# The direct term of the first half on VectorE, and the scan ahead of the second inverse chain: an S5 block on Trainium2

## The reference, cut to what matters

```python
x = x + _L0_conv_ref(_gn(x), ...)          # x: (16, 96, 16, 16), float32; _gn: 32 groups of 3 channels

def _L0_conv_ref(x, ...):
    u = x.reshape(Bsz, C, H * W).transpose(0, 2, 1)
    fx = _layernorm(u, ln1_g, ln1_b)                        # over the 96 channels
    res = fx
    ...                                                     # lam_bar, B_bar, masked Cc from 48 complex modes
    Bu = jnp.einsum('ph,blh->blp', B_bar, fx)
    _, xs = jax.lax.associative_scan(binop, (lam_el, Bu), axis=1)      # a linear recurrence over 256 positions
    y = 2.0 * jnp.real(jnp.einsum('hp,blp->blh', Cc, xs)) + D * fx
    y = jax.nn.gelu(y, approximate=False) + res
    fy = _layernorm(y, ln2_g, ln2_b)
    z = fy @ W_enc.T
    z1, z2 = jnp.split(z, 2, axis=-1)
    z = z1 * jax.nn.gelu(z2, approximate=False)
    y = z @ W_dec.T + fy
    return y.transpose(0, 2, 1).reshape(Bsz, C, H, W)
```

## Time and profile before

| | |
|---|---|
| median of 3 runs | 106.98 us |
| the profiled execution's own time | 106.55 us |
| its span, first to last instruction | 104.6 us |
| mean granted clock of TensorE | 0.991 |
| busy: PE, DVE, ACT, POOL | 95.2, 71.0, 43.8, 38.8 us |

### The profile page before, as it was taken

One profiled execution on the slowest core, in us unless ns is written; L12 is line 12 of the kernel. 1 busy time (PEld: TensorE's weight loads), 2 busy tenths in 40 slices (PEclk: granted clock), 3 DMA queues, 4 the chain that ended last, 5 costly groups with the idle time before them and its releaser, 6 DMA issues.

```text
span 104.6 us, 1481 instructions
## 1 busy us (share of the span) xinstructions
PE 95.2 (91%) x496; PEld 54.9 (52%) x496; DVE 71.0 (68%) x220; ACT 43.8 (42%) x93; POOL 38.8 (37%) x54
## 2 busy tenths in 40 slices
PE   5999789799999998898999999996899999999960
PEld 3667468274676654764775655674232533533300
DVE  1596995998670998585839113699950599994590
ACT  3420099999768001010292069254079322025200
POOL 7710465910599920000047000038992000495000
PEclk9999999999999999999999999999999999999996
DMA  2999100000000000000000000000000000550125
GB/s 76 250 247 217 24 0 0 0 6 0 3 0 0 0 0 6 0 0 0 0 3 0 0 0 0 6 0 0 0 0 0 0 0 0 150 151 6 51 79 171
DMA packets 3767, 3.79 MB, mean 36 GB/s; under 512 B 496, under 2 KB 3664, under 8 KB 3760
## 3 DMA queue, kind: packets, MB, share of 16 engines
q1 hardware_dynamic: 3504, 3.68, 13.8%
q10 hardware_dynamic: 256, 0.02, 0.2%
HBM read 2.12 MB, written 1.57 MB: 35 GB/s over the span
## 4 chain that ended last, share of the span: by engine, by line
PE 53%; DVE 19%; ACT 11%; DMA 6%; issue 5%; SPq 2%; DVEq 1%
PE ps L495 53%; DMA xs<-x_dram 6%; ACT xc L406 4%; ACT sq L406 3%; DVE w L744 3%; DVE rs L744 3%; ACT rotC L393 2%; DVE upper L748 2%; DVE fy L744 2%; SPq L247 1%; DVE rs L774 1%; DVE sq L744 1%; DVE st L783 1%; DVE y L1012 1%; DVE rs L749 1%
## 5 line engine op out<-in xcount | busy, mean ns | idle before, releaser
L343 POOL TENSOR_TENSOR y<-gl,fx 96x512 f32<-96x512 f32 x4 | 6.6, 1666 | 29.4 <-ACT gl L446 29.4
L495 PE MATMUL ps<-fy,mt 96*96 96x512 f32 x32 | 14.9, 599 | 1.3 <-DVE fy L744 1.3
L351 POOL TENSOR_TENSOR res<-fy,xs 96x512 f32<-96x512 f32 x8 | 10.7, 1354 | 11.6 <-DVE fy L744 11.5
L495 PE MATMUL ps<-wm 96*96 96x256 f32 x42 | 13.0, 467 | 1.2 <-DVE wm L980 1.2
L452 ACT ACTIVATE y<-ps,vecs 96x512 f32<-96x512 f32 x8 | 5.5, 685 | 16.5 <-PE ps L495 16.5
L744 DVE SCALAR_TENSOR_TENSOR w<-ps,vecs,y 96x512 f32<-96x512 f32 x8 | 5.9, 743 | 7.4 <-ACT y L452 7.4
L495 PEld LDWEIGHTS ps<-wm 96*96 96x96 f32 x42 | 8.2, 205 | 4.2 <-DVE wm L980 1.2
L495 PEld LDWEIGHTS ps<-fy,mt 96*96 96x96 f32 x32 | 5.0, 163 | 8.7 <-issue 6.9
L495 PE MATMUL ps<-xs,pm 96*96 96x256 f32 x32 | 8.5, 393 | 1.0 <-DVE pm L832 1.0
L744 DVE SCALAR_TENSOR_TENSOR w<-w,tb,ps 96x256 f32<-96x256 f32 x14 | 6.6, 472 | 3.8 <-ACT w L432 3.1
L495 PE MATMUL ps<-fx,dm 96*96 96x512 f32 x16 | 8.3, 602 | 0.4 <-DVE Z L880 0.4
(11 more groups left out here) (120 smaller groups left out, 161.9 us busy)
## 6 DMA issues: line engine op xcount, KB each, us to landing
out_dram<-sq SPq DMA_DIRECT2D x8, 192.0 KB, 2.2
xs<-x_dram SPq DMA_DIRECT2D x3, 384.0 KB, 6.5
xs<-x_dram SPq DMA_DIRECT2D x2, 192.0 KB, 2.9
mt<-mats_dram SPq DMA_DIRECT2D x1, 338.6 KB, 7.5
mt<-mats_dram SPq DMA_DIRECT2D x1, 180.0 KB, 5.2
sm<-small_dram ACTq DMA_DIRECT2D x1, 8.6 KB, 2.9
cmask<-mask_dram ACTq DMA_DIRECT2D x1, 9.0 KB, 3.1
```

What stands on the lines that cost most here:

```text
L343: nc.gpsimd.tensor_tensor(yv[:, RT * i:RT * (i + 1), :], cols(gl, H, i).rearrange("c (b m) -> c b m", b=RT), cols(fx, H, i).rearrange("c ( ...
L351: nc.gpsimd.tensor_tensor(cols(res, H, i), cols(fy, H, i), xs[:, HB * H + 2 * i:HB * H + 2 * i + 2, :].rearrange("c n l -> c (n l)"), ALU. ...
L495: return nc.tensor.matmul(o, lhsT, rhs, start=start, stop=stop)
```

## The change

Four edits. (1) A Sin activation of one column comes ahead of ScalarE's first copy. (2) `first_state(0)` moves ahead of the six centred copies. (3) The seven scan steps of the first half run in a row ahead of the second half's inverse chain. (4) The first half's four `direct` products go, the first local product of a tile now starts the accumulation, and `direct_term` on VectorE computes `fx * D + bank` into `gl`, from which Gelu then reads in place; the four multiply-adds stand among the second half's scan steps.

```diff
@@ -368,8 +370,9 @@
             act.dma_start(sm[:, :], small).then_inc(in_small, 16)
             act.dma_start(cmask[:, :], mask_in).then_inc(in_mask, 16)
+            act.wait_ge(wm_ready, 1)
+            nc.scalar.activation(sn[:, :], wm[:, 0:1], ACT.Sin)
             act.wait_ge(in_mask, 16)
@@ -442,8 +445,11 @@
                 act.wait_ge(db_ready, 1)
                 for i in range(NT):
-                    act.wait_ge(y_done, NT * H + i + 1)
-                    nc.scalar.activation(cols(gl, H, i), bank(H, i)[0:96, :], ACT.Gelu,
+                    if H:
+                        act.wait_ge(y_done, NT + i + 1)
+                    else:
+                        act.wait_ge(y_direct, i + 1)
+                    nc.scalar.activation(cols(gl, H, i), bank(H, i)[0:96, :] if H else cols(gl, H, i), ACT.Gelu,
                                          bias=db[:, 0:1]).then_inc(gl_ready, 1)
@@ -473,9 +479,9 @@
             squares(1, 4, HB)
-            centered_values(1, 2, HB)
             act.wait_ge(ones_ready, 2)
             first_state(0)
+            centered_values(1, 2, HB)
             seed(0)
@@ -605,7 +611,7 @@
                     mm(bank(H, i)[0:96, RC * j:RC * (j + 1)], yl[:, 0, b, :], rcols(w, H, b),
-                       start=False, stop=False)
+                       start=(H == 0 and j == 0), stop=False)
@@ -686,14 +692,14 @@
             for i in range(NT - 1):
-                direct(0, i)
+                pe.wait_ge(w_local[0], RT * (i + 1) - 1)
                 local_outputs(0, i)
...
-            direct(0, NT - 1)
+            pe.wait_ge(z_ready, NDBL)
             local_outputs(0, NT - 1)
@@ -878,6 +884,12 @@
+            def direct_term(i):
+
+                dve.wait_ge(y_done, i + 1)
+                stt(cols(gl, 0, i), cols(fx, 0, i), s(DD), bank(0, i)[0:96, :],
+                    ALU.mult, ALU.add).then_inc(y_direct, 1)
@@ -1015,9 +1027,10 @@
-            scan(0, 1)
-            scan(0, 2)
-            inverse_sigma(0, 1, lambda j: scan(0, j + 3) if 0 <= j < T - 3 else None)
+            for b in range(1, T):
+                scan(0, b)
+            inverse_sigma(0, 1)
+            dve.wait_ge(taken[0], 2 * HB)
             scale_tile(0, 1, 0, fx, s(G1), fx_ready)
@@ -1025,6 +1038,9 @@
             for b in range(1, T):
                 scan(1, b)
+                if b % 2 and b > 1:
+                    direct_term(b // 2 - 1)
+            direct_term(NT - 1)
             second_input(0, 1)
```

More of the change, by code:

```diff
@@ L122, in s5_block @@
         wm = sb("wm", [96, WARM_N])
+        sn = sb("sn", [96, 1])
         pm = sb("pm", [96, B, 96])
@@ L190, in s5_block @@
         y_done = sem("y_done")
+        y_direct = sem("y_direct")
         gl_ready = sem("gl_ready")
```

## The result

The changed kernel takes 108.15 us (median of 6 runs, 107.24 to 116.46), the kernel before 106.97 (6 runs, 106.52 to 109.21). The ratio is 1.0101, interval 1.0056 to 1.0146: slower by about 1%, by less than 2%. The profiled execution took 107.24 us, span 105.2, against 106.55 and 104.6.

A forecast was written before the change was run, and what follows sets the result against it. TensorE was taken as the main bound, with VectorE's chain setting the second half's broadcast. Chain gain -0.7 and multiply-adds +0.5 sum to -0.2 us, from 106.55 to 106.3 us; range 105.4 to 108.6.

The forecast's parts named there:

- rival A: TensorE's idle hole near 38 to 41 us lowers its clock: 2.0 us lost, 108.3 us in all; chance 0.30.
- the cost of the hole: Three direct products removed beside the chain save nothing; broadcast to last doubling stays 6.9 us at full clock.
- Table and first state: Front: one table load of 1.28 us goes, state copy moves ahead of six copies; first scan at 32.0, not 33.83.
- `rotS` near 24.1: Front: TensorE's `rotS` product starts 0.8 us earlier, near 24.1 instead of 24.95.
- Hold by GpSimd: Second inverse chain: its second link waits for GpSimd's last product in flight, until 37.47 as before.
- `parts` 41.15: Second inverse chain ends at 41.15 instead of 41.87, 3.68 us after the held second link.
- the term of -0.7: Gain of 0.7 us up to the end of the second inverse chain, from 41.87 to 41.15.
- The hole of 3.3 us: TensorE idles 3.3 us ahead of the second half's broadcast, near 37.9 to 41.2, where it idled 0.57.
- The multiply-adds, +0.5: First outputs: four VectorE multiply-adds among the scans delay `seed_sum` to 54.3 from 53.82, losing the 0.86 saved too.
- cover: First outputs: time from the end of `second_input` to the centring shrinks from 1.9 to 1.2 us and holds.
- Rivals B: GpSimd doesn't hold the second inverse chain: gain there 1.4 us instead of 0.7, 105.6 us; chance 0.13.
- C: First Gelu's tail is late, so the centring waits for `y2`: 106.8 us at 0.5 over the cover; chance 0.07.

The follow-up runs named there:

- experiment 1: Changed kernel plus six warm-up products in TensorE's hole ahead of the second half's broadcast: 106.54 us, ratio to before 0.9966.
- experiment 2: Changed kernel plus three warm-up products in TensorE's hole, about 1.9 us of it left: 107.74 us, ratio to before 1.0045.
- experiment 4: Kernel before with only the multiply-adds in place of the direct products: ratio to before 1.0055 from five of twelve executions; median of all twelve 108.68 us.
- experiment 7: Changed kernel with direct products back on TensorE and GpSimd's last product waiting for the second half's `parts`: 105.49 us, ratio to before 0.9861.
- experiment 9: Changed kernel plus six warm-up products in the hole and the four multiply-adds behind all seven second-half scans: 106.51 us, ratio to before 0.9946.
- experiment 6: Kernel before with only the first half's scans in one go: ratio to before 1.0035.
- experiments 5: Kernel before with only the early sine table and early first state: ratio to before 0.9932, from four of six executions.
- the repeat of 7: Same kernel again, direct products on TensorE and GpSimd's last product delayed: 105.21 to 113.87 us in 6 runs, no ratio given.

## Why the prediction was wrong

The forecast, 106.3 us and slightly faster, was wrong in its sign; what happened is rival A.

**The step that failed** is the cost of the hole. The sum says of the removed products that they "save nothing and open a hole", and puts the hole at nothing: "from the broadcast to the last doubling 6.9 us as now". That stage measured 7.92 us (before 6.85), a loss of 1.07 against a forecast sum of -0.2, and 6.92 once the hole was filled (experiment 1). The reason given for leaving it out, and for the chance of 0.30, was that "one fall at the end of a kernel, with a half-busy second ahead of it, is thin evidence". But the fall is no rare event: none of the changed kernel's six executions had a mean clock above 0.984, where 25 of 66 of the kernel before in these runs were that low; it came behind 1.90 us too (experiment 2), and even with pieces of at most 1.2 us (experiment 4). The earlier trace rows had shown the fall after some 1.6 us; that row should have carried the forecast. The rule of the Trainium skill (TensorE: Matmul & The Clock Gate, Why this matters for your kernels), that idle gaps between bursts put the clock back, had been cited for rival A. The runs agree with it in direction; but the gaps of experiments 2 and 4 are shorter than those that the page warns of, and there the measurement decides.

**Rival A's price** was taken as 2.0 us, from a range of 1.3 to 2.6. The traces show two sizes: 1.07 where the low clock lasted from 40.95 to 44.4 (the changed kernel), and 2.55 where it lasted for most of seven microseconds (experiment 4). Over the runs, the ratios 1.0101 and 0.9966 of the changed kernel and of experiment 1 differ by 1.3%, or 1.4 us: near the lower bound. That rival A's 108.3 lies so near the measured median of 108.15 is in part luck: its sum is 1.8 us above the profiled execution's 106.55, which is itself 0.4 below the median of before, and the measured rise is 1.01%, or 1.1 us. The length of the low level had been guessed from the slow passes at the start; the granted clock reads 1.00 from 0 to 8 us, so those passes alone speak for it.

**The other terms held.** Table and first state: one table load fewer, predicted first scan 32.0, measured 32.16 (with this execution 0.14 late). `rotS` near 24.1: 24.33. Hold by GpSimd: second link let go at 37.47 predicted, 37.61 measured, and experiment 7 shows that the product is its cause. `parts` 41.15 predicted, 41.27 measured; the term of -0.7 measured -0.75. The hole of 3.3 us measured 3.21. The multiply-adds, +0.5, measured +0.22: `seed_sum` was let go by the seventh scan as foreseen, but the loss was over-counted. The scans ended 5.35 us into the stage (54.59 - 49.24), not the 5.47 reckoned; and I compared the wait's end with the start of the weight load before, 53.82, which ran 0.22 ahead of its product (54.04), where now both start at 54.64. `second_input` had more cover than reckoned: 1.6 instead of 1.2 us.

**Rivals B and C** did not come: the link was held, and the centring did not wait for `y2` (it does in experiment 9).

Where I had given the scan order a share of the 0.7, experiment 6 corrects it: in the kernel with the late front it is worth nothing, since first scan to end of `parts` takes the same 8 us either way. With the early front the ratios, 0.9932 without it and 0.993 with it, show no share either.

## What to carry to other kernels

Work that lies beside another engine's chain is not free to remove when TensorE does it: it may be what keeps the clock up. Before taking products out of a stretch in which TensorE waits, count the idle time this leaves there, in one piece or several, and put in fillers or other work. And where one link of a VectorE chain is several times as long as its like, look which GpSimd instruction ends at that moment, and move that one.

## What I had not expected of the hardware

The clock fell with no idle stretch over 1.2 us (experiment 4), and in the front of three traces (experiments 5, 6 and the repeat of 7) a microsecond or two behind waits of 0.8 us or less, where other executions with the same waits kept it. Which executions fall, and what starts the falls of the front, stays open. The same kernels ran single executions at 0.88 to 0.97 of mean clock on these chips, with up to 9 us more, and one at 0.54 throughout that took 164.19 us, although TensorE was busy for 89.62 of the 90 us from 10 to 100. A scan step with one operand in PSUM lasted 0.47 us beside GpSimd's product, and a 96x512 multiply-add 0.74 with GpSimd idle and 0.70 beside it, while links of the inverse chain with SBUF operands alone waited for the end of GpSimd's whole product (0.85 to 1.18 us instead of 0.22 to 0.29).
